# Causal self-attention in a decoder kernel: softmax numerators split in SBUF and transposed by DMA

## The reference

```
q = einsum('bsd,hqd->bhsq', x, w_q)        # k, v alike; x is layer-normed
scores  = einsum('bhsq,bhtq->bhst', q, k)
masked  = where(triu(ones, k=1), -inf, scores)
weights = softmax(masked / sqrt(64))
out     = einsum('bhst,bhtv->bhsv', weights, v)
cat     = out.transpose(0, 2, 1, 3).reshape(b, s, 1024)
return einsum('bsf,df->bsd', cat, w_o)     # added to x
```

## Time and profile before

| quantity | value |
|---|---|
| median of the runs | 3410.08 us |
| profiled execution, first to last instruction | 3421.4 us |
| TensorE busy (matmul / weight load) | 2765.8 us (81%) / 2326.6 us (68%) |
| VectorE busy | 2121.3 us (62%) |
| ScalarE busy | 1500.5 us (44%) |
| GpSimd busy | 554.3 us (16%) |
| mean granted TensorE clock | 0.868 of full speed |
| transposes `l_turn` (L1133) | 2304 |
| DMA moved | 77.48 MB, mean 23 GB/s |

### The profile page before, as it was taken

One profiled execution on the slowest core, in us unless ns is written; L12 is line 12 of the kernel. 1 busy time (PEld: TensorE's weight loads), 2 busy tenths in 40 slices (PEclk: granted clock), 3 DMA queues, 4 the chain that ended last, 5 costly groups with the idle time before them and its releaser, 6 DMA issues.

```text
span 3421.4 us, 68444 instructions
## 1 busy us (share of the span) xinstructions
PE 2765.8 (81%) x25142; PEld 2326.6 (68%) x25142; DVE 2121.3 (62%) x4697; ACT 1500.5 (44%) x2901; POOL 554.3 (16%) x392
## 2 busy tenths in 40 slices
PE   4677999977667799997767779999766778999985
PEld 4566888855556688875555678888545667888754
DVE  5564656667566466666756646666675655666667
ACT  1323666622322466662332256666133226666523
POOL 0111222201001122121101022221100102222110
PEclk7679999978688999997967799999796789999978
DMA  3001111100000111110000011110000011111000
GB/s 96 1 27 26 35 25 37 26 15 1 14 1 27 29 32 37 25 27 15 1 14 1 27 32 35 31 37 15 15 1 14 1 32 37 25 37 31 16 0 13
DMA packets 43074, 77.48 MB, mean 23 GB/s; under 512 B 6778, under 2 KB 27642, under 8 KB 42874
## 3 DMA queue, kind: packets, MB, share of 16 engines
q1 hardware_dynamic: 34106, 66.52, 7.7%
q10 hardware_dynamic: 8768, 8.39, 0.8%
HBM read 37.14 MB, written 4.19 MB: 12 GB/s over the span
## 4 chain that ended last, share of the span: by engine, by line
PE 46%; issue 27%; DVE 14%; ACT 5%; POOL 4%; DMA 2%; DVEq 1%; ACTq 1%; SPq 0%; POOLq 0%
PE ps L1154 8%; PE ps L210 6%; PE ps L1133 6%; PE ps L212 6%; PE ps L211 6%; PE ps L1122 3%; PE ps L1123 3%; ACT l_pe L1245 2%; DVE l_pt L1374 2%; PE ps L1106 2%; ACT l_pt L1255 2%; POOL c_pn L924 2%; DVE nmax L1367 1%; PE ps L1505 1%; PE ps L1522 1%
## 5 line engine op out<-in xcount | busy, mean ns | idle before, releaser
L1374 DVE TENSOR_TENSOR l_pt<-ps,l_pt 128x512 f16<-128x512 f32 (+3 forms) x768 | 404.0, 554 | 470.1 <-ACT l_pt L1255 463.9
L1133 PE MATMUL ps<-idf,l_pe 128*128 128x128 f32 x2304 | 357.9, 284 | 130.8 <-ACT l_pe L1245 107.2
L1367 DVE TENSOR_REDUCE nmax<-ps 128x1 f32<-128x1024 f32 (+7 forms) x512 | 381.5, 746 | 116.3 <-PE ps L1124 115.6
L1255 ACT CAST l_pt<-ps 128x512 f16<-128x512 f32 (+3 forms) x768 | 344.7, 482 | 233.9 <-PE ps L1133 173.1
L1154 PE MATMUL ps<-l_v,l_pt 128*128 128x64 bf16 x11520 | 442.6, 197 | 0.0
L1154 PEld LDWEIGHTS ps<-l_v,l_pt 128*128 128x128 f16 x11520 | 429.6, 101 | 12.0
L1245 ACT ACTIVATE l_pe<-ps,nmax 128x1024 f32<-128x1024 f32 (+7 forms) x512 | 385.9, 754 | 12.1 <-DVE nmax L1367 10.1
L1133 PEld LDWEIGHTS ps<-idf,l_pe 128*128 128x128 f32 x2304 | 267.9, 145 | 180.7 <-DVE l_pt L1374 143.0
L1122 PE MATMUL ps<-l_k,l_q 128*128 128x512 f32 (+3 forms) x768 | 306.4, 399 | 1.4 <-DMA l_k<-l_k 1.4
L1446 POOL TENSOR_TENSOR l_k<-l_ks,l_k 64x1024 fp32r<-64x1024 f32 x64 | 152.4, 2381 | 681.6 <-ACT l_k L1264 681.6
L1123 PE MATMUL ps<-l_k,l_q 128*128 128x512 f32 (+3 forms) x768 | 259.1, 349 | 0.0
(11 more groups left out here) (315 smaller groups left out, 6709.9 us busy)
## 6 DMA issues: line engine op xcount, KB each, us to landing
l_k<-l_k SPq DMA_DIRECT2D x128, 256.0 KB, 3.5
l_w<-in_l_w SPq DMA_DIRECT2D x32, 384.0 KB, 3.6
xin<-in_x SPq DMA_DIRECT2D x4, 1024.0 KB, 5.6
m_w<-in_m_w SPq DMA_DIRECT2D x8, 512.0 KB, 4.3
m_w<-in_m_w SPq DMA_DIRECT2D x4, 1024.0 KB, 8.2
l_wo<-in_l_wo ACTq DMA_DIRECT2D x32, 128.0 KB, 2.6
out_x<-x ACTq DMA_DIRECT2D x4, 1024.0 KB, 5.0
s_g<-in_g_wg SPq DMA_DIRECT2D x1, 1024.0 KB, 4.9
```

Of the source, the lines that this page charges most:

```text
L1133: last = pe.transpose(o, L["l_pe"][:, k % 2, j * P:(j + 1) * P], idf[:])
L1255: s.copy(L["l_pt"][:, k % 2, 0, here], ps[:, 4 + j, 0:here.stop - here.start]).then_inc(q_["p1"], 1)
L1367: v.tensor_reduce(nmax[:, k % 2:k % 2 + 1], banks_of(k)[:, 0:(i + 1) * P], AX.X, ALU.max, negate=True).then_inc(q_["max"], 1)
L1374: v.tensor_tensor(L["l_pt"][:, k % 2, 1, here], ps[:, 4 + j, 0:here.stop - here.start], L["l_pt"][:, k % 2, 0, here], ALU.subtract).then_i ...
```

## The change

The numerators no longer go through TensorE and PSUM. ScalarE casts `l_pe` to f16 into a new SBUF tile `l_ph` (upper part, one instruction per row tile), VectorE subtracts it from `l_pe` into the other half of `l_ph` (lower part), and SyncE issues one DMA transpose per row tile, of both parts (2(i+1) blocks of 128x128 f16), into `l_pt`. `l_ph` and `l_pt` have NS = 4 slots; `l_pe` still has two. Scores and maxima run AHEAD = 5 tiles ahead of the products, exponentials 4, the split and the DMA 3. One reciprocal per head (in `l_finish`) takes the place of one per row tile. Banks 4 and 5, free now, take the projections of the next pair, which also move to earlier steps. The weights of the next pair are loaded from inside SyncE's new loop over row tiles, and the key copies sit between transposes there.

```diff
+NS = 4
+AHEAD = 5
...
-            ("l_pe", [P, 2, T], F32), ("l_pt", [P, 2, 2, T], F16), ("l_o", [P, NT, P], F32),
+            ("l_pe", [P, 2, T], F32), ("l_ph", [P, NS, 2 * T], F16), ("l_pt", [P, NS, 2 * NT, P], F16), ("l_o", [P, NT, P], F32),
...
+        def turned(it, k):
+            return q_[f"pt{k % NS}"], (it * (NB1 // NS) + k // NS + 1) * 16
...
-        def l_turn(pe, it, k, first=False):
-            ...
-                last = pe.transpose(o, L["l_pe"][:, k % 2, j * P:(j + 1) * P], idf[:])
...
         def l_pv(pe, it, k, first, more):
...
-            pe.wait_ge(q_["p2"], it * NP1 + parts(k + 1))
+            pe.wait_ge(*turned(it, k))
...
         def l_pe_body(pe, it, first, more):
             for k in range(NB1):
-                if k + 1 < NB1 or more:
-                    l_turn(pe, it, k + 1)
+                if k + AHEAD < NB1 or more:
+                    l_score(pe, it, k + AHEAD)
                 l_pv(pe, it, k, first, more)
-                if k + 3 < NB1 or more:
-                    l_score(pe, it, k + 3)
+                if more and k in (1, 2):
+                    if k == 1:
+                        pe.wait_ge(q_["wl"], it + 3)
+                    l_proj(pe, 1, k - 1, 3 + k, q_["k"])
...
+                if more and k in (3, 4):
+                    pe.wait_ge(q_["ks"], it * 2 + k)
+                    l_proj(pe, 0, k - 3, k + 1, q_["q"])
+                if more and k in (6, 7):
+                    pe.wait_ge(q_["qs"], it * 2 + k - 3)
+                    l_values(pe, k - 6, k - 2)
...
         def l_exp(s, it, k, first=False):
...
             if not (first and k < 2):
-                s.wait_ge(q_["tp"], it * NP1 + parts(k - 1))
-                s.wait_ge(q_["rc"], it * NB1 + k - 1)
+                s.wait_ge(q_["lo"], it * NB1 + k - 1)
...
+        def l_upper(s, it, k, first=False):
+            _, i = bl1[k % NB1]
+            n = (i + 1) * P
+            s.wait_ge(q_["exp"], it * NB1 + k + 1)
+            if not (first and k < NS):
+                s.wait_ge(*turned(it, k - NS))
+            s.copy(L["l_ph"][:, k % NS, 0:n], L["l_pe"][:, k % 2, 0:n]).then_inc(q_["hi"], 1)
...
         def l_a_body(s, it, hp, first, more):
             for k in range(NB1):
-                l_upper(s, it, k, first)
-                if k + 1 < NB1 or more:
-                    l_exp(s, it, k + 1, first)
+                if k + 4 < NB1 or more:
+                    l_exp(s, it, k + 4, first)
+                if k + 3 < NB1 or more:
+                    l_upper(s, it, k + 3, first)
...
-                if more and k == 1:
+                if more and k == 0:
                     s.wait_ge(q_["v"], it * 2 + 2)
                     l_w_a(s, it + 1)
...
         def l_lower(v, it, k):
+            v.wait_ge(q_["hi"], it * NB1 + k + 1)
+            v.tensor_tensor(L["l_ph"][:, k % NS, n:2 * n], L["l_pe"][:, k % 2, 0:n], L["l_ph"][:, k % NS, 0:n],
+                            ALU.subtract).then_inc(q_["lo"], 1)
...
         def l_v_body(v, it, first, more):
             for k in range(NB1):
-                l_lower(v, it, k)
-                l_inverse(v, it, k, first)
-                if k + 2 < NB1 or more:
-                    l_max(v, it, k + 2)
+                if k + AHEAD < NB1 or more:
+                    l_max(v, it, k + AHEAD)
+                if k + 3 < NB1 or more:
+                    l_lower(v, it, k + 3)
                 if not first and k == 0:
                     l_finish(v, it - 1, 1)
-                if more and k == 1:
+                if more and k == 0:
                     l_w_v(v, it + 1)
...
+                if more and k == 14:
+                    l_query_lower(v, it + 1, 1)
                 if not first and k >= 12:
                     g = k - 12
                     v.wait_ge(q_["wo"], it * 4 - 3 + g)
...
+        def l_flip(sp, it, k, first=False):
+            sp.wait_ge(q_["lo"], it * NB1 + k + 1)
...
+                sp.wait_ge(q_["pv"], it * NB1 + k - NS + 1)
...
+            sp.dma_start_transpose(L["l_pt"][:, k % NS, 0:2 * (i + 1), :], L["l_ph"][:, k % NS, 0:2 * n]).then_inc(q_[f"pt{k % NS}"], 16)
...
+        def l_sp_body(sp, it, hp, first, more):
+            for k in range(NB1):
+                if more and k == 0:
+                    l_load_w(sp, it + 1, hp + 1)
+                if k + 3 < NB1 or more:
+                    l_flip(sp, it, k + 3, first)
+                if more and k == 7:
+                    l_dup(sp, it + 1, 0)
+                if more and k == 14:
+                    l_dup(sp, it + 1, 1)
```

More of the change, by code:

```diff
@@ L1143, in l_pv @@
                 pe.wait_ge(q_["v3"], it * 2 + 2)
-                if more:
-                    pe.wait_ge(q_["qs"], it * 2 + 4)
-                else:
+                if not first:
                     pe.wait_ge(q_["oh"], it * 2)
-            pe.wait_ge(q_["p2"], it * NP1 + parts(k + 1))
+            pe.wait_ge(*turned(it, k))
             o = ps[:, 6 + h, i * SD:(i + 1) * SD]
@@ L1242, in l_exp @@
             if not (first and k < 2):
-                s.wait_ge(q_["tp"], it * NP1 + parts(k - 1))
-                s.wait_ge(q_["rc"], it * NB1 + k - 1)
+                s.wait_ge(q_["lo"], it * NB1 + k - 1)
+            if not (first and k < NB1) and i == NT - 1:
+                s.wait_ge(q_["rc"], (it + k // NB1) * 2 + h - 1)
             s.activation(L["l_pe"][:, k % 2, 0:n], banks_of(k)[:, 0:n], ACT.Exp, bias=nmax[:, k % 2:k % 2 + 1],
-                         accum_out=sums[:, k % 2:k % 2 + 1]).then_inc(q_["exp"], 1)
-        def l_upper(s, it, k, first):
-            _, i = bl1[k]
-            if not (first and k < 2):
-                s.wait_ge(q_["pv"], it * NB1 + k - 1)
-            for j in range(banks_in(i)):
-                here = part_cols(i, j)
-                s.wait_ge(q_["tp"], it * NP1 + parts(k) + j + 1)
-                s.copy(L["l_pt"][:, k % 2, 0, here], ps[:, 4 + j, 0:here.stop - here.start]).then_inc(q_["p1"], 1)
+                         accum_out=lsum[:, h, i:i + 1]).then_inc(q_["exp"], 1)
+        def l_upper(s, it, k, first=False):
[5 more added lines that the diff above has]
+            s.copy(L["l_ph"][:, k % NS, 0:n], L["l_pe"][:, k % 2, 0:n]).then_inc(q_["hi"], 1)
         def l_w_a(s, n):
@@ L1769, in _ @@
                 m_sp(sp, b)
-                with sp.Fori(0, HP) as hp:
-                    l_sp_body(sp, b, hp)
+                l_sp_first(sp, b)
+                l_sp_body(sp, b * HP, 0, True, True)
+                with sp.Fori(1, HP - 1) as hp:
+                    l_sp_body(sp, b * HP + hp, hp, False, True)
+                l_sp_body(sp, b * HP + HP - 1, HP - 1, False, False)
             sp.wait_ge(s_out, 16 * B + 16)
```

164 lines of the change are left out of this document (68 added, 96 removed).

## The result

The changed kernel took 3772.05 us (median of 4 runs, 3762.34 to 3779.4), the kernel before on the same chip 3410.44 us (4 runs). The ratio is 1.105, with a 95% interval of 1.1023 to 1.1074. The forecast was slower, 3690 us, in a range of 3480 to 4250; it was 362 us that were added, not 277. The profiled execution after took 3779.4 us, with a span of 3777.6.

The account below looks back on a forecast made before the run. TensorE was taken as the bound within a pair. 17.1 + 29.1 + 6.3 + 5 = 57.5 us against 50.76 gave +189 over 28 steps, with +32 entering batches and +56 clock: 3410 + 277, say 3690 us, range 3480 to 4250.

Parts of the forecast that it names:

- the prediction's own signs: Observations named beforehand as showing it right, among them a period of 55 to 60 us and a tail near 17 us.
- Term 1, the ring of the tail: Pair's tail: output projection, scores, maximum, split, addition run serially; four steps sum to 17.1 us against 13.57 before.
- 2 us per pair for the clock: Whole pair: allowance for a lower granted TensorE clock at 67% busy, +56 us in all.
- Term 2, the weights: Before the next pair's key projection: weights load behind a waiting transpose, stalling TensorE 2.3 + F + Q, taken as 6.3 us.
- time Q: Weights load's wait behind the transpose's own 384 KB in the DMA engines: between nothing and 4.8 us, taken as 2.
- Term 3: Second head's large tiles 8 to 11: ring of exponential, cast and split falls short; 0 to 8 us, taken as 5.
- 29.1 us for the head without waits: Pair outside its tail: 37.2 us less 6.0 of transposes and 2.1 of idle time, if nothing else waited.
- 50 ns per piece: DMA engines: the dearer price for 256-byte pieces, 57.6 us per pair, against 18.7 at plain rate, held likelier.
- Entering a batch: Start of each batch: three transposes wait for each other, 0 to 15 us, taken as 8, four times, +32 us.
- The DMA-bound case: Rival: 256-byte pieces make the DMA engines the bound, 74 us per pair, 4120 us in all; chance 0.23.
- the one block by block: Rival: each transpose waits for every block separately, about 7800 us or over 15,000 us in all; chance 0.04.
- "Faster": Rival: TensorE's transposes were the bound and nothing replaces them; 47.2 us per pair, 3310 us; chance 0.09.

Follow-up runs that it names:

- e1: Changed kernel with VectorE's addition of an output-projection part ahead of the step's maximum and split: 3613.12 us, 159 us saved.
- e2: Changed kernel with the next pair's weights loaded a whole pair earlier in SyncE's queue: 3631.55 us, 140 us saved.
- e8: Changed kernel with 21 filler products of 512 columns per pair on TensorE, ahead of its waits in the tail: 3724.76 us.
- e3: Changed kernel without the DMA transposes, products reading the split numerators untransposed (does not compute the reference): 3562.0 us.
- e7: Changed kernel with GpSimd's lower parts of keys and values on a sixteenth of their columns from a batch's second pair on (work left out): 3649.44 us.
- e6: Changed kernel with only the order swapped: ScalarE casts k+3 before exponential k+4, VectorE splits k+3 before maximum k+5: 3407.38 us.
- e4: Changed kernel with the edits of e1, e2 and e6 together: 3241.17 us, 0.9501 of the kernel before.

## Why the prediction was right, and where its sizes were not

**Direction and mechanism: right.** TensorE loses its transposes, two waits take their place, and e1 and e2 show both by taking them away: 159 and 140 us, 329 together. Two of the prediction's own signs did not come as stated: the period is 62.9 us, not 55 to 60, and the tail from the first `l_out` to the next pair's first product is 21.7 us (16.4 + 5.3), not near 17.

**Term 1, the ring of the tail.** In kernels whose clock stays at full in the tail (e8, and most of e3 and e7) its first three steps take 4.0, 4.7 and 5.7 us, against 3.74, 4.42 and 5.28 in the sum: 1.0 us was missing, of handoffs most likely. In the run after, the 14 tails whose small split runs free take 15.2 us, 0.8 more, at a lower clock. The 10 whose small split lies beside a GpSimd instruction take 18.8; of their further 3.6 us the split itself is some 1.1, and the rest goes with a lower clock (0.78 in the mean, 0.86 in the 14). In the pair shown, one of these, the four steps are 6.32, 6.13, 6.97 and 5.23 us. The fourth step takes 5.3 us in the mean, not 3.66. The forecast had 2 us per pair for the clock, in the whole pair, and nothing for VectorE's splits waiting beside GpSimd, a cost that e7 puts at up to 122 us.

**Term 2, the weights.** Over-sized: the stall was 4.2 us in the mean of 28 and 3.07 in the pair shown (1444.58 in the timeline), not 6.3. The issue of the transpose took 1.41 us and not 2, no time Q behind it shows (the weights landed within 3.5 us of their issue), and TensorE came later itself, because its scores and products ran at a lower clock (35 weight loads of the products took 2.01 us there, 40 of them 1.22 just before).

**Term 3: the step that failed.** The prediction charged 5 us for the ring of exponential, cast and split, in tiles 8 to 11 only, held it to fit beside the steps of the tail, and charged nothing elsewhere. Its 29.1 us for the head without waits is borne out within 2.1 us: in e6, where the ring is undone, head and stall take 36.3 us less 3.7 for the fourth step, 32.6, of which 1.4 is stall. After the change they take 46.5 - 5.3 = 41.2 us, with 3.8 of stall in these pairs. So 41.2 - 29.1 - 3.8 = 8.3 us were lost where the sum had 5. A part of the 8.3 is the clock, 0.82 in the rest after and 0.94 in e6; no run separates it. The waits of ScalarE in the pair of the timeline say why:

```profile
ACT l_pe L1212 <- DVE l_ph L1345: 19.6, 13, 3.8
```

13 of 16 exponentials wait for a split (total us, times, longest): four in the tail and nine behind it, where the forecast charged four tiles. With two buffers of numerators, exponential k+5 needs the split of k+3. That split stands behind the maximum of k+5, which needs scores, and behind a cast that stands behind exponential k+4. So a split whose numerators are long ready waits for scores, a maximum and an exponential that it doesn't need, and the next exponential waits for it. The clearest place is where the second head begins (timeline of ScalarE and VectorE):

```profile
1454.48 1.12 ACT L1212 ACTIVATE l_pe<-ps,nmax 128x1024 f32<-128x1024 f32 x1 [1.56 <-DVE nmax L1339]
...
1455.58 0.29 ACT L1221 CAST l_ph<-l_pe 128x128 f16<-128x128 f32 x1
...
1455.91 1.09 DVE L1339 TENSOR_REDUCE nmax<-ps 128x1 f32<-128x896 f32 x1 [1.52 <-PE ps L1120]
1456.92 2.51 DVE L1345 TENSOR_TENSOR l_ph<-l_pe,l_ph 128x128 f16<-128x128 f32 x1
...
1459.52 1.01 ACT L1212 ACTIVATE l_pe<-ps,nmax 128x896 f32<-128x896 f32 x1 [2.21 <-DVE l_ph L1345]
```

From one exponential to the next 5.04 us pass, for a cast and a split of 128 columns whose numerators were ready before the first of the two began. 2.2 of the 5.04 us are the wait beside GpSimd (the split takes 2.51 us, not 0.28); the others are the order. TensorE's page rows don't name this wait: it shows there as scores that wait for an exponential (118.8 us at L1118) and as work spread thin. The forecast's ring in the head had exponential, cast and split in it, 3.4 us for a tile of 1024 columns, but neither the maximum that stands ahead of the split nor the scores that it needs, and it looked for the ring at the large tiles alone.

**The DMA engines.** The choice of plain rate over 50 ns per piece was right. 151.06 MB more in 16 x 737.6 us of engine time is 205 GB/s, against the 253 of q1 before. The Trainium skill ("Advanced Engine Details and Errata", X-Bar Transpose) has transposing DMAs on this chip as fast as regular ones; the trace agrees within a fifth, and packets of 256 bytes took 19.5 ns with the transposes and 18.0 ns in q1 before (768 of them). The 1309 ns that the Trainium skill ("VectorE: DVE Perf Modes", The three transpose paths) lists for one block did not add up block by block: 144 blocks take 22.5 us of each engine's time in a pair, 0.16 us per block. Who waited for a transpose, over the whole run: TensorE for 15.9 us at its weight loads.

**Entering a batch and the sum.** The forecast had 28 equal steps at 6.7 + 2 us, 245 us, and 32 for entering the batches. Measured are 319 us in the 28 steps and 37 outside them, of which the way from a batch's first exponential to its ninth has 5 (26.0 us before, 27.3 after); the others can't be placed more closely. In the 20 middle steps the sum was 3.4 us short of 62.9: the tail by 2.6 (21.7 for 17.1 + 2), head and stall by only 0.8 (41.2 for 40.4). That 0.8 is luck: the weights' stall was set 2.5 us too high there and the ring 3.3 too low. That the total came within 85 us of the measured 362 rests on this in part.

**The rivals.** The DMA-bound case fell (share 0.44), and so did the one block by block. "Faster" did not come, and e4 shows why it was not absurd: the work taken from TensorE is worth it when the order allows (3241 us).

## What to carry to other kernels

When work leaves the busiest engine, follow every in-order engine through one step and write down which buffer each instruction waits for; a ring through two engines that are busy 40% and 58% can set the pace, and its waits stand on rows of those engines, not on TensorE's. Put what frees a buffer (cast, split, addition) ahead of what fills the next one; here that alone was worth 365 us and with the two other moves 531. A load that nobody waits for today belongs ahead of any transfer in the same queue that waits for computed data.

## What the runs showed of the hardware

- A VectorE subtraction with both operands in SBUF is held while a GpSimd tensor instruction runs that began first: splits of 128 columns took 1.36, 1.9 and 2.51 us instead of 0.28, and 0.42 with GpSimd thin (e7). In the run after, 98 subtractions with both operands in SBUF overlapped a GpSimd tensor instruction that had begun first, and none ended before it. The split at 1456.92 above lies beside this instruction of GpSimd:

```profile
1456.90 2.37 POOL L1415 TENSOR_TENSOR l_k<-l_ks,l_k 64x1024 fp32r<-64x1024 f32 x1 [13.18 <-ACT l_k L1230]
```

It began 0.02 us before the split and ended 0.16 us before it. The Trainium skill ("SBUF — State Buffer", SBUF: two separate sides) calls the shared port pair an exclusive lock that a VectorE operation with two SBUF inputs contends for with a GpSimd operation that reads SBUF; the trace agrees, and the change, by moving the split's input from PSUM to SBUF, walked into it. Thinning GpSimd's work was worth 122 us of 3772 (e7), the clock's part in it included.
- A DMA transpose holds SyncE's queue for 1.17 to 2.63 us at its issue (median 1.28) against 0.46 of a plain copy, and lands in 2.3 to 6.9 us (median 3.2).
- With 21 extra products per pair in the tail, the granted clock of its first three steps was 0.98 in the mean instead of 0.83, and that of the rest 0.79 instead of 0.82 (e8), for a gain of 47 us, not all of it the clock's. Where TensorE was busy 38 of 43 us (e4), it was 1.00 throughout the pair shown.
